# The diagonal constant of a matrix polynomial, added by four products in 32 by 32 tiles of TensorE instead of one product over 512 columns

## The reference

```python
def newtonschulz5(G, steps=NS_STEPS):          # NS_STEPS = 2
    a, b, c = (3.4445, -4.775, 2.0315)
    X = G.astype(jnp.bfloat16)
    X = X / (jnp.linalg.norm(X, axis=(1, 2), keepdims=True) + 1e-07)
    for _ in range(steps):
        A = X @ X.transpose(0, 2, 1)
        Bm = b * A + c * (A @ A)
        X = a * X + Bm @ X
    return X
```

## Time and profile before

| | us |
|---|---|
| median of 3 runs | 1576.62 (1576.53 to 1580.05) |
| the profiled execution, whole | 1579.73 |
| its span in the trace | 1578.0 |
| TensorE busy in the span | 1453.2 (92%) |
| VectorE busy | 1255.5 (80%) |
| ScalarE busy | 1008.8 (64%) |
| GpSimd busy | 860.6 (55%) |

### The profile page before, as it was taken

One profiled execution on the slowest core, in us unless ns is written; L12 is line 12 of the kernel. 1 busy time (PEld: TensorE's weight loads), 2 busy tenths in 40 slices (PEclk: granted clock), 3 DMA queues, 4 the chain that ended last, 5 costly groups with the idle time before them and its releaser, 6 DMA issues. The chain is left out here.

```text
span 1578.0 us, 44161 instructions
## 1 busy us (share of the span) xinstructions
PE 1453.2 (92%) x12447; PEld 995.9 (63%) x12543; DVE 1255.5 (80%) x4299; ACT 1008.8 (64%) x2284; POOL 860.6 (55%) x996
## 2 busy tenths in 40 slices
PE   7994789999999999999963799999999999999996
PEld 4663578788888888888852355555555555555774
DVE  4663578999999999999955687777777777774998
ACT  4773477777777777777741466666666666662221
POOL 1332345688888888888877244444444444442333
PEclk9996799999999999999965899999999999999998
DMA  3875335455655553333224567677667666624995
GB/s 121 257 237 172 113 121 160 148 174 177 193 178 176 173 159 93 99 95 115 87 91 158 158 199 203 195 205 213 194 196 210 196 199 199 189 72 107 264 267 136
DMA packets 264982, 264.40 MB, mean 168 GB/s; under 512 B 87467, under 2 KB 236312, under 8 KB 264752
## 3 DMA queue, kind: packets, MB, share of 16 engines
q1 hardware_dynamic: 204464, 176.51, 38.8%
q0 software_dynamic: 19968, 51.16, 8.9%
q10 hardware_dynamic: 40320, 33.96, 8.7%
HBM read 142.70 MB, written 122.98 MB: 168 GB/s over the span
## 5 line engine op out<-in xcount | busy, mean ns | idle before, releaser
L1749 POOL DMA_INDIRECT scratch_y<-eo,goes x224 | 225.8, 1008 | 340.5 <-ACT eo L1843 294.0
L1774 PE MATMUL e_psGU<-wexp,e_xT 128*64 x896 | 291.2, 468 | 0.2 <-issue 0.2
L1776 PE MATMUL e_psGU<-e_up,e_xT 128*64 128x352 f32 x896 | 291.1, 468 | 0.0
L1381 POOL DMA_INDIRECT scratch_buf<-rows,dest x180 | 194.5, 1080 | 49.1 <-issue 39.7
L1864 ACT ACTIVATE e_up<-wexp 128x704 f32 x224 | 177.0, 790 | 26.9 <-issue 26.9
L1774 PEld LDWEIGHTS e_psGU<-wexp,e_xT 128*64 128x64 f32 x896 | 114.0, 137 | 122.4 <-issue 122.4
L1984 DVE COPY e_down<-wexp 128x512 f32 x224 | 93.9, 419 | 92.9 <-PE e_psD L1799 89.6
L1843 ACT ACTIVATE eo<-e_psD 128x256 f32<-128x256 f32 x224 | 85.5, 384 | 87.2 <-issue 46.7
L1391 POOL TENSOR_TENSOR f_wnr<-f_wss,f_half 128x4 f32<-128x4 f32 x96 | 98.5, 1035 | 59.0 <-DVE f_wss L1194 58.5
L1832 ACT ACTIVATE e_sgm<-e_psGU 128x176 f32<-128x176 f32 x224 | 71.1, 318 | 78.5 <-PE e_psGU L1776 64.6
L1793 PE MATMUL e_psD<-wexp,e_hT 112*64 x448 | 115.5, 379 | 1.6 <-DVE e_hT L1939 1.6
(11 more groups left out here) (339 smaller groups left out, 4366.6 us busy)
## 6 DMA issues: line engine op xcount, KB each, us to landing
e_xg<-scratch_buf ACTq DMA_DIRECT2D x436, 66.0 KB
scratch_y<-f_blank SPq DMA_DIRECT2D x64, 384.0 KB
c_g<-scratch_y SPq DMA_DIRECT2D x64, 384.0 KB, 8.4
scratch_qkvT<-q_tT SPq DMA_DIRECT2D x16, 768.0 KB, 5.0
wexp<-in_wgT SPq DMA_DIRECT2D x64, 176.0 KB, 3.2
wexp<-in_wuT SPq DMA_DIRECT2D x64, 176.0 KB, 3.3
scratch_buf<-f_blank SPq DMA_DIRECT2D x65, 132.0 KB, 2.0
scratch_kv<-q_y SPq DMA_DIRECT2D x16, 512.0 KB, 2.8
```

The costliest lines, as they stand in the source:

```text
L1381: pool.indirect_dma_start(out=T["buf"], out_offset=bass.IndirectOffsetOnAxis(dest[:, i, k:k + 1], 0), in_=rows[:, i % RR, :], in_offset=No ...
L1749: pool.indirect_dma_start(out=T["y"], out_offset=bass.IndirectOffsetOnAxis(goes[:, n:n + 1], 0), in_=eo[:, n % OB, :], in_offset=None, bou ...
L1774: pe.matmul(psGU[0:RT, n % 2, 0:2 * F], xT[:, n % 4, k, 0:RT], ring[:, bass.ds(at[n] + k * 2 * F, 2 * F)], start=(k == 0), stop=(k == KD - 1))
L1776: mm = pe.matmul(psGU[RT:P, n % 2, 0:2 * F], xT[:, n % 4, k, RT:P], up2[:, n % 2, k * 2 * F:(k + 1) * 2 * F], start=(k == 0), stop=(k == K ...
```

## The change

`polynomial` now begins with `beta_i^T A`, which opens the bank with `start=True`. The constant comes second: four products, one for each 32 by 32 block on the diagonal of the array. Block `own` takes rows `own` and columns `own` of `gamma_l` as weights, and moves the `own` partitions of `gamma_r`, in each of the four matrices only the columns `own`: 4 x 32 = 128 columns. It writes partitions `own`, and there only the columns in which the constant lies. `A A` follows as before. Tables, waits, evictions and the order of steps stay as they are.

```diff
             def polynomial(a, x, m):
                 dst = bank(x, m)
-                pe.matmul(flat(dst), gamma_l[:, :], flat(gamma_r[:, :, :]), start=True, stop=False)
-                pe.matmul(flat(dst), beta_i[:, :], flat(a[:, x, m, :, :]), start=False, stop=False)
+                pe.matmul(flat(dst), beta_i[:, :], flat(a[:, x, m, :, :]), start=True, stop=False)
+                for low in range(0, P, 32):
+                    own = slice(low, low + 32)
+                    pe.matmul(dst[own, :, own], gamma_l[own, own], gamma_r[own, :, own], start=False, stop=False)
                 for q in range(Q):
                     mm = pe.matmul(dst[:, q, :], a[:, x, m, q, :], a[:, x, m, q, :], start=False, stop=(q == Q - 1))
                 return mm
```

## The result

The changed kernel takes 1581.94 us (median of 15 executions, 1579.59 to 1588.06); the kernel before, on the same chip, 1576.62 (1574.98 to 1580.05). The ratio is 1.0037 [1.0027, 1.0047]: 5 to 6 us slower. The direction was forecast, the size was not: +5.3 us by the medians against +13.2. (In the experiments two single executions, one of e13 at 1725 us with a mean granted clock of 0.825 and one of e16 at 1880 us with 0.737, stand apart from their kernels' others and enter no ratio.)

The account below looks back on a forecast made before the run. TensorE and VectorE were taken as matched. Each polynomial adds 0.302 us and saves 0.216, 16.5 us over 192; less 3.3 absorbed, +13.2 on 1576.6 gives 1589.8 us, range 1579 to 1620.

Parts of the forecast that it names:

- What bounds the kernel now: Polynomial stage: TensorE and VectorE matched, TensorE with little more than 0.1 us to spare in a 19.5 us half iteration.
- What the change removes: One 512-column product in each polynomial: 0.216 us of TensorE's time, 41.5 us over 192 polynomials.
- What it adds: Four 128-column tile products and two changes of tile in each polynomial: 0.302 us of TensorE's time.
- For 32 columns of bfloat16 I take half, 0.025: Loading the first tile's weights after the change into tiles: 0.025 us a polynomial, half the 0.05 for 64 float32 columns.
- 3 x 0.007: Later starts of the other three tiles, in us, on top of 0.056 for 128 columns, giving 0.077.
- the prediction's sign: What the changed profile should show: first `A A` product starting 0.52 us after `beta_i`.
- What moves: TensorE falls back 0.52 us a half iteration, 0.12 absorbed; 16.5 less 3.3 gives +13.2 us for the kernel.
- wait for `dg`: TensorE's wait before the first gradient product, taken as 0.12 us a half iteration, which the change should use up.
- nothing to measure: Rival: cheaper changes of tile or more hidden by VectorE's pace make both sides equal, 1576.6 to 1581 us; chance 0.08.
- The four take turns: Rival: the tile products, writing one PSUM bank, run one after another; +41.4 us, 1618 us; chance 0.17.
- Changes of tile are cheap here: Rival: changes of tile in mid-polynomial could be hidden, TensorE gains; about -5 us, 1571.6 us; chance 0.07.
- the case I had thought likeliest: Tiles side by side, changes of tile at full price: 1589.8 us, own range 1585 to 1597; chance 0.68.

Follow-up runs that it names:

- e13: Kernel before plus an overwritten whole-array product of 64 columns at the head of each polynomial: 1579.18 us, ratio 1.0009.
- e16: The kernel before, unedited, run again for a profile on an ordinary chip: 1577.74 us, ratio 1.0002.
- experiment 2: Kernel before with the constant left out of every polynomial, and no tiles: 1572.59 us, ratio 0.9966.
- e9: The kernel before, unedited, run again for a profile on another ordinary chip: 1577.57 us, ratio 0.9995.
- e10: The changed kernel, unedited, run again with a profile on another ordinary chip: 1581.03 us, ratio 1.0027 to the kernel before.
- experiment 5: Changed kernel with the four tile products issued twice in each polynomial: 1590.72 us, ratio 1.0081 to the kernel before.
- experiment 4: Kernel before with the constant cut to one tile of one column, after the beta_i product: 1577.68 us, on another chip 1577.26.
- e8: The changed kernel again, on a second chip where the kernel before takes 1659.5 us: 1699.67 us, ratio 1.0216.
- e15: Kernel before with the constant cut to one tile of one column, on another ordinary chip: 1577.26 us, ratio 0.9999.
- e3: Kernel before plus an overwritten whole-array product of 128 columns at the head of each polynomial: 1583.27 us, ratio 1.0034.
- e11: Kernel before plus an overwritten whole-array product of 128 columns in each polynomial, on another chip: 1582.77 us, ratio 1.0031.

## Why the prediction was right in direction and wrong in size

**"What bounds the kernel now": right in the main.** The two engines are matched, TensorE does not set the pace, and it had about 0.13 us to spare (forecast 0.12; "little more than 0.1"). "One that gives it less is hardly rewarded" is experiment 2. "Paid for nearly in full" was too strong for so small an addition: of 0.324 us in a half iteration, 0.18 were paid.

**"What the change removes": right,** 0.216 us.

**"What it adds": this step failed, in two of its terms.** Forecast 0.095 + 0.025 + 0.077 + 0.105 = 0.302; measured 0.093 + 0 + 0.066 + 0.101 and 0.010 at the second `A A`, 0.270.

- "For 32 columns of bfloat16 I take half, 0.025": measured 0. The first load was counted twice. The 0.095 for the way in was read from start to start, 511.22 to 511.54 in the earlier trace rows, with the first tile's load of 64 float32 columns already in it. The 0.05 from which I scaled stands inside that group, between its first pair of passes and its second (511.54 and 511.70, 0.154 apart where later pairs are 0.11 apart), and not at the change of tile.
- The spread of the four: "3 x 0.007" from row halves 0.01 apart; measured 0.010 in all, 3 to 4 ns each. The Trainium skill, "TensorE: Matmul & The Clock Gate", Part 3, has about 4 ns a tile, and on this the trace agrees. The price of going in and out, 0.194 us by the rows, decided the sign.

The two come to 0.025 + 0.011; the way in was 0.002 too dear and the way out, with the later start of the second `A A`, 0.006 too cheap. In all that is 0.032 us a polynomial, 192 x 0.032 = 6.1 us too many. From `beta_i` to the first `A A` it is 0.476 us, where the prediction's sign was 0.52. It is a difference of two nearly equal numbers, 0.302 - 0.216: an error of a tenth in the first makes one of more than a third in the result.

**"What moves": this step had the first wait right, and failed in what is absorbed and in the path.** The net work is 192 x 0.054 = 10.4 us, and 4.6 us reach the end, so 5.8 are absorbed, where I had 3.3 and had called 3.8 the most. By the copies of e9 and e10, the last 25 half iterations were given 8.1 us and grew by 3.5, the first six 1.9 and grew by 1.1. The wait for `dg` went at each of the steady half iterations, and a usual one absorbed 0.14 us. The "0.12" had been read from two places (0.13 and 0.12); the same rows held 0.21 at a third, and a half iteration that had taken 20.3 us before, the longest of the full stretch, took 20.2 after. The wait that replaced it stands at ScalarE's squares (L1196): the prediction let ScalarE "issue what it did" and looked for the delay at VectorE's update, but it came through ScalarE's queue. Of the 13.2 us forecast, 6.1 go with the price of the tiles and 2.5 with what is absorbed, which leaves the 4.6 of the pair of profiles; the 2.5 is itself worked out from that 4.6, so the sum is a division of the miss and no second proof. The times say 3.1 and 5.3 us by the medians, 4.3 and 5.8 by the ratios.

That the time lies within the range at all, by 3 us, is owed to a range that takes in part of "nothing to measure", and not to the sum.

**The rivals.** "The four take turns" is refuted by experiment 5 and by the 0.23 us of the group. The rule of the Trainium skill that stood for it, "TensorEngine Tiling (Array Packing)", Gotcha 1, that different row tiles cannot access one bank at the same time, is not borne out by these rows for tiles that write different partitions of it: four start within 0.010 us. "Changes of tile are cheap here" is refuted by experiment 4, while its second half, that the kernel would get little of a saving, is confirmed by experiment 2 (5 us for the largest possible saving). "Nothing to measure" was nearer than the case I had thought likeliest: its "1576.6 to 1581" is missed by 0.9 us here and by 0.03 in e10, and the interval begins at 0.27%, within the 0.3% that I had set. What it missed is that the difference is real. Its point was right: I had put too little slack on TensorE's side. It had been given 0.08, which was too little for a case that only needed two small terms to err the same way.

## What to carry to other kernels

An excursion into tiles of TensorE's array costs two changes, 0.19 to 0.20 us together, before any column is moved, so one with four tiles of 128 columns side by side, 0.27 us, takes less of TensorE's time only where it replaces more than that, or where several things share one excursion. Before charging or crediting an engine's time, find the pace of the other engine by steps that occur once a round: here 1.3 us less of TensorE's work in a half iteration was worth nothing once the stage was full (and 5 us in all at its start), and the first 0.13 us more would, by the line drawn back, cost next to nothing. A delay can also reach the engine that sets the pace through the queue of a third one, so the lists of waits of all of them are to be read. Where the answer is the difference of two nearly equal costs, the small terms decide its size; each deserves its own bounds in the range of the likeliest case.

## What the runs showed of the hardware that was not expected

- A tile of one column costs 0.197 us between whole-array products, and four diagonal tiles of 128 columns only 0.07 more. The first tile's weights (87 ns in the trace) add nothing that shows.
- A stretch of 7 to 10 us at 1.2 GHz, beginning at 227 to 230 us, occurred in 3 of the 7 profiles of kernels with tiles (the first of the change, e8 and e15) and in none of the 11 without. In e15, whose time is unchanged, the rows read as in the changed kernel:

```profile
228.65 3.62 PE L924 MATMUL spare<-f_qT,f_Wn 128*128 128x64 f32 x16
```

  It costs 3.0 to 4.3 us where it occurs. With so few profiles I don't call the link to the tiles shown. Single times point the same way. Of the 27 executions of the change on ordinary chips seven took over 1585 us, and the four over 1586.9, the profiled one among them, all have a mean granted clock of 0.953, where the usual ones have 0.957 to 0.960. None of the 14 with 128 columns more (e3 and e11), whose ratios are alike, took over 1584.4, and those of the kernel before end at 1581.5 but for the one of 1880. Why the clock fell stays open.
- One chip ran the same kernel in 1659.5 us where three others needed 1577, and set the kernels in another order. All four profiles there have a granted clock below 1.00 from 200 to 790 us, lower with tiles (0.88, 0.89) than without (0.95 twice). A few tenths of a per cent, measured on one chip, say nothing of such a one.
